# Moving the tile-pair sum of squares and one residual add from VectorE to GpSimd

## What is computed

```python
def _rfs(xw, ab, AB, gs):
    dot_products = jnp.einsum('...d,rd->...r', xw, ab[:, None] * gs)
    correction = (0.5 * jnp.sum(xw * xw, axis=-1))[..., None] * (ab * ab)
    return 1.0 / math.sqrt(NUM_RFS) * AB * jnp.exp(dot_products - correction)
...
    weights = _rfs(input_weights, ab, AB, proj_matrix)
    feats = _rfs(x, ab, AB, proj_matrix)
    return jnp.einsum('bsr,or->bso', feats, weights)
...
    real = jnp.einsum('bti,io->bto', x, jnp.cos(theta + theta_noise))
    imag = jnp.einsum('bti,io->bto', x, jnp.sin(phi + phi_noise))
    return jnp.sqrt(real * real + imag * imag)
...
x = _layernorm(x + _L0_attn_ref(x, L0_attn_input_weights, L0_attn_xis, L0_attn_proj_matrix), axis=-1)
x = _layernorm(x + _L0_ffn_ref(x, L0_ffn_theta, L0_ffn_phi, L0_ffn_theta_noise, L0_ffn_phi_noise), axis=-1)
```

## Time and profile before

| | us |
|---|---|
| median of 3 runs | 764.39 (762.92 to 764.94) |
| the profiled execution, its own time | 764.39 |
| its span, first to last instruction | 762.6 |
| PE matmul busy | 719.6 (94%) |
| VectorE busy | 604.6 (79%) |
| ScalarE busy | 490.7 (64%) |
| GpSimd busy | 175.1 (23%) |
| mean granted TensorE clock | 0.986 of 2.4 GHz |

### The profile page before, as it was taken

How to read it: one execution, slowest core, us unless ns; L and a number is a source line. 1 busy time by engine, 2 the same in 40 slices (tenths; PEclk the granted TensorE clock), 3 DMA queues, 4 the chain that set the end, 5 groups by cost and what they waited for, 6 DMA issues and landing times. The chain is left out here.

```text
span 762.6 us, 10949 instructions
## 1 busy us (share of the span) xinstructions
PE 719.6 (94%) x3228; PEld 583.8 (77%) x3228; DVE 604.6 (79%) x1009; ACT 490.7 (64%) x758; POOL 175.1 (23%) x419
## 2 busy tenths in 40 slices
PE   9989996799999999999999999999999999999892
PEld 7867885687878878787887878788787878788771
DVE  5898784778787797888788887878889787887876
ACT  6837545484866848485775858577585848665453
POOL 5772120210304031120403022040402203040311
PEclk9999999799999999999999999999999999999997
DMA  9752004140313114040321314032221403110001
GB/s 292 207 123 69 1 32 137 40 138 15 117 63 110 57 39 138 14 144 35 110 69 37 128 29 150 14 110 69 80 85 41 138 14 115 63 55 0 28 28 55
DMA packets 32754, 60.81 MB, mean 80 GB/s; under 512 B 3168, under 2 KB 3168, under 8 KB 32736
## 3 DMA queue, kind: packets, MB, share of 16 engines
q1 hardware_dynamic: 31584, 58.50, 23.0%
q0 software_dynamic: 1152, 2.10, 1.6%
HBM read 43.78 MB, written 16.81 MB: 79 GB/s over the span
## 5 line engine op out<-in xcount | busy, mean ns | idle before, releaser
L772 PE MATMUL token_ps<-W_hi,F_hi 128*128 128x512 f32 x256 | 102.5, 400 | 12.8 <-ACT late L574 9.1
L391 POOL TENSOR_TENSOR var_eps<-mv,eps 128x2 f32<-128x2 f32 x29 | 5.9, 204 | 466.6 <-DVE mv L1072 466.6
L636 ACT ACTIVATE late<-late 128x1024 f32<-128x1024 f32 x56 | 56.5, 1053 | 78.8 <-DVE late L1355 77.7
L773 PE MATMUL token_ps<-W_lo,F_hi 128*128 128x512 f32 x256 | 100.8, 394 | 0.0
L774 PE MATMUL token_ps<-W_hi,F_lo 128*128 128x512 f32 x256 | 100.6, 393 | 0.0
L720 PE MATMUL project_ps<-xT_hi,gs_hi 128*128 128x512 f32 x248 | 100.1, 404 | 0.4 <-DVE expo L979 0.4
L722 PE MATMUL project_ps<-xT_hi,gs_lo 128*128 128x512 f32 x248 | 97.1, 392 | 0.0
L721 PE MATMUL project_ps<-xT_lo,gs_hi 128*128 128x512 f32 x248 | 96.7, 390 | 0.0
L555 ACT ACTIVATE late<-late 128x1024 f32<-128x1024 f32 x29 | 30.8, 1061 | 71.6 <-DVE late L1123 71.6
L772 PEld LDWEIGHTS token_ps<-W_hi,F_hi 128*128 128x128 f32 x256 | 48.7, 190 | 28.2 <-issue 9.5
L974 DVE TENSOR_TENSOR zT_lo<-turn_ps,zT_hi 128x512 fp32r<-128x512 f32 x64 | 35.3, 569 | 38.2 <-ACT zT_hi L616 29.6
(11 more groups left out here) (210 smaller groups left out, 1816.4 us busy)
## 6 DMA issues: line engine op xcount, KB each, us to landing
x_tok<-in_x SPq DMA_DIRECT2D x16, 1024.0 KB, 5.4
out_tokens<-o_tile SPq DMA_DIRECT2D x64, 256.0 KB, 2.1
plain_xT_lo<-in_xT SPq DMA_DIRECT2D x14, 1024.0 KB, 5.3
norm_bc<-token_norms SPq DMA_DIRECT2D x15, 256.0 KB, 3.1
plain_T_hi<-in_gsT SPq DMA_DIRECT2D x4, 256.0 KB, 4.8
z<-in_wT SPq DMA_DIRECT2D x4, 256.0 KB, 5.3
plain_T_lo<-in_xT SPq DMA_DIRECT2D x1, 1024.0 KB, 7.9
plain_T_hi<-in_theta SPq DMA_DIRECT2D x4, 256.0 KB, 6.0
```

Of the source, the lines that this page charges most:

```text
L636: nc.scalar.activation(parts[:, p, i, :, :], parts[:, p, i, :, :], ACT.Square).then_inc(square_done, 2)
L772: nc.tensor.matmul(o, F_hi[:, c, cols], W_hi[:, c, :], start=(c == 0), stop=False)
L773: nc.tensor.matmul(o, F_hi[:, c, cols], W_lo[:, c, :], start=False, stop=False)
```

## The change

pair_sum moves from DVE to POOL for both pairs, with the same operands and semaphores; only the last block's pair 1 stays with DVE. pair_residual2 moves to POOL for pair 0; for pair 1 it stays on DVE. POOL runs pair_sum(b - 1, 1) ahead of its other work of block b, and pair_sum(b, 0) and pair_residual2(b, 0) behind it. On DVE the first statistics of pair 0 (pair_stats2(b, 0, 0)) move ahead of the joins C21 and C12.

```diff
@@ POOL
+            def pair_sum(b, p):
+                pool.wait_ge(square_done, 2 * C * b + C * p + C + SQUARE_CREDIT)
+                pool.tensor_tensor(parts[:, p, :, 0, :], parts[:, p, :, 0, :], parts[:, p, :, 1, :], ALU.add).then_inc(sum_made, 2)
+
+            def pair_residual2(b, p):
+                pool.wait_ge(mag_made, C * b + 2 * p + 2)
+                pool.tensor_tensor(parts[:, p, :, 0, :], z[:, 2 * p:2 * p + 2, :], parts[:, p, :, 0, :], ALU.add).then_inc(y2_made, 2)
...
+            pair_sum(1, 0)
+            pair_residual2(1, 0)
 
             def step(b):
+                pair_sum(b - 1, 1)
                 pair_scale2(b - 1, 0)
                 scale1(b, 0)
                 scale1(b, 1)
                 pair_scale2(b - 1, 1)
                 scale1(b, 2)
                 scale1(b, 3)
+                pair_sum(b, 0)
+                pair_residual2(b, 0)
@@ DVE, second_step
-                pair_sum(b, 0)
                 split_columns(b + 2, 0)
                 split_sums(3)
-                pair_residual2(b, 0)
                 split_columns(b + 2, 1)
                 pair_stats2(b, 0, 0)
@@ DVE, step, head of the block
                 stats1(b, 0)
-                pair_sum(b - 1, 1)
                 stats1_made(b, 0)
@@ DVE, step, pair 1
                     join_v(1)
-                    pair_sum(b, 0)
                     if ahead:
                         split_columns(b + 2, 1)
                     join_c22(1)
                     join_w(1)
                     join_c11(1)
-                    pair_residual2(b, 0)
+                    pair_stats2(b, 0, 0)
                     join_c21(1)
                     join_c12(1)
-                    pair_stats2(b, 0, 0)
                     return
```

More of the change, by code:

```diff
@@ L1118, in next_exponent @@
                 exponent(C * (b + 2) + j, j, slot, project_ps[j % 2], j % 2)
[L1121 to L1127, removed]
             def pair_stats2(b, p, i):
@@ L1283, in second_step, with pair_residual2 @@
                 split_sums(2)
-                pair_sum(b, 0)
                 split_columns(b + 2, 0)
                 split_sums(3)
-                pair_residual2(b, 0)
                 split_columns(b + 2, 1)
                 pair_stats2(b, 0, 0)
+            def pair_residual2(b, p):
+                dve.wait_ge(mag_made, C * b + 2 * p + 2)
+                tt(parts[:, p, :, 0, :], z[:, 2 * p:2 * p + 2, :], parts[:, p, :, 0, :], ALU.add).then_inc(y2_made, 2)
             def step(b, pair, slot, more, ahead):
```

## The result

The changed kernel takes 797.9 us (median of 4 runs, 797.2 to 798.2); the kernel before, on the same chip, takes 764.1 us (762.9 to 764.9). The ratio is 1.044, 95% interval 1.042 to 1.046. The direction of the forecast held; the size did not: 783.7 us was forecast, 792 was the end of the range. The profiled execution took 797.25 us, with a span of 795.4 us against 762.6 before, so 32.8 us have to be accounted for.

A forecast was written before the change was run, and what follows sets the result against it. PE was taken as the bound, waiting at block boundaries for DVE's join C11. Twelve boundaries at +1.65 us (+19.8) less 0.5 in the last block gave +19.3 on 764.39, or 783.7 us; own range 778 to 790, wider range 776 to 792.

The forecast's parts named there:

- The boundary: Blocks 2 to 13: two split_columns held up by POOL's adds make join C11 late, 12 x 1.65 = +19.8 us.
- the second race: Before join C11: POOL's residual starts 0.32 us before split_columns half 1 and holds it up, +1.94 us per boundary.
- rival A: At the boundary, POOL's residual starts after split_columns half 1: 760.3 us; 756.7 us without any exclusion; chance 0.12.
- rival B: At each boundary PE's longer wait lowers the granted clock: 12 x 2.0 adds 24 us, 808 us; chance 0.04.
- The 2.2 us row: At 117 to 125 us, a 2.2 us PE wait left the clock at 1.00; taken as evidence against rival B.
- Step (3): Between blocks 1 and 2: 1.2 us more for POOL's sum ends inside ACT's 5.1 us transfer wait, costing nothing.
- block 14: No further block is loaded and no split_columns runs beside POOL, so PE should not wait for its join: no cost.
- step (1): Block head: POOL's sum of pair 1 stays hidden, since PE's transpose leaves 4.0 us and the sum takes 2.4.
- Last block: No split_columns here, and the removed work stood before the last joins: -0.5 us.

The follow-up runs named there:

- both orders: The change, with both split_columns moved behind join C11 of pair 1 and join C11 of pair 0 ahead of the last features' split: 760.9 us.
- the kernel with block 1 on VectorE: Against the change, only the sum and residual of pair 0 of block 1 go back to VectorE: 795.5 us, ratio 1.042.
- small matmuls: The change with 8 unread 128x128 identity matmuls before PE's boundary waits of blocks 3 to 14: 785.3 us; with 14 of them, 794.8 us.

## Why the prediction was wrong in size

**The boundary, right.** +1.65 us each was forecast from the one-column, the 128x512 and the start-up rows; 1.69 was measured. POOL's adds took 2.41 and 2.39 us where 2.4 was put, the splits 2.1 and 3.2 us as forecast. PE's idle time is 2.0 us instead of 1.95. The lead that decided the second race was 0.30 us for 0.32. The experiment with the delayed residual shows that the order is the cause, and that rival A was the right description of the other side: 760.3 us by A, 762.5 with the 2.2 us between blocks 1 and 2, 762.9 measured. POOL's busy time grew by 94.8 us and not by 106: its adds took the 106.4 us, but the rest of its work 11.6 us less, which was not looked into.

**The clock, wrong; the failed step is the dismissal of rival B.** "The 2.2 us row speaks against it" rested on one wait, in one place, behind which the clock had stayed at 1.00. Behind twelve waits of 1.9 to 2.0 us it fell seven times. Equal waits with equal work around them went both ways, so the length of a wait does not decide alone, and one row could not exclude a fall. Even the same place went both ways. That wait is 1.8 to 2.3 us in all 14 kernels here; the clock stayed at 1.00 in ten of them, the kernel before and the change included, and fell in four. The kernel before, and the one that moves only the sum of pair 1:

```profile
120.55 0.47 PE L800 MATMUL token_ps<-zT_hi 128*128 128x512 f32 x1 [2.19 <-ACT late L574]
```

```profile
121.46 0.77 PE L805 MATMUL token_ps<-zT_hi 128*128 128x512 f32 x1 [2.31 <-ACT late L579]
```

In the second the granted clock of 121 to 125 us is 0.57. The forecast should have counted a fall behind a good part of the 12 boundaries. Rival B's price was too high (2.0 us each, taken from behind a wait of 9.1 us; 1.6 measured), as was its count (12; 7 measured). B's half, 11.3 us, is the largest part of the miss.

**Between blocks 1 and 2, wrong.** Step (3) looked only at the chain through the squares and let the sum end inside ACT's wait. It did not ask which of VectorE's operations the sum would meet, nor what ends that wait. The end of the wait is a load behind stores in SP's queue, and the stores wait for what the sum held up. This is the second step that failed: a term put at 0; 2.2 us by the comparison of executions, 1.9 in this one.

**Block head and block 14, right.** PE meets neither the sum of pair 1 nor block 14, in the change and in the experiment with that sum alone. The cover that step (1) named is of this kernel, however: with both orders changed, VectorE's expo comes 1.45 us late and PE waits for it, so its cover there is less than the 4.0 us of the transposes.

**Last block, right.** -0.5 was forecast, -0.8 measured. How it comes about was not looked into; with the sum of pair 0 alone the same stretch is 0.5 us longer.

## What to carry to other kernels

Before an operation goes from VectorE to GpSimd, list every SBUF operation of VectorE that will run in its time, whichever chain it belongs to, and follow each to the queue behind it; an operation may move to an engine with time to spare and still lengthen the path of the one that it left. When a wait of TensorE grows from some tenths of a us to about 2 us, count a possible fall of the clock in the range and not as a remote rival, unless many rows of such waits exclude it; a single row that shows none is little evidence. And look first at the order on the engine that is waited for: here two orders on VectorE gave 13 us, while every variant with the sums on GpSimd was slower than its partner or equal to it.

## What was not expected of the hardware

- Waits of 2.0 us lowered TensorE's granted clock behind 7 of 12 boundaries (8 of 12 in the kernel with block 1 on VectorE), those of 0.84 us behind none of 12, and idle times of 0.22 us between small matmuls and the mix behind none. A wait of 2.2 us in the kernel before had not. In the change the falls follow the order none, fall, fall; in the kernel with block 1 on VectorE there are never two boundaries without a fall in a row, and never three with one. What sets this order was not tried; it is open.
- VectorE's TENSOR_SCALAR on one SBUF tile (two of 128x512) is held up by GpSimd's add as well: 3.09 us instead of 1.00. The rows of the start-up showed this for two SBUF inputs only. The Trainium skill, page SBUF — State Buffer, section SBUF: two separate sides, counts VectorE operations in a 2-port mode, beside those with two SBUF inputs, among those that take the shared ports. The trace does not show the mode; the hold-up agrees with it, and the prediction had not applied it.
- The lead of 0.12 us that the earlier trace rows showed for a 128x512 add holds up VectorE for the rest of a 128x1024 add too (2.39 us; 312.00 against 312.12).
